# A transformer layer (linear attention, then eight experts) on one core, with every engine's calls in another order

## The reference, cut to what matters

```python
x = x + attn(layernorm(x), w_qkv, w_out)      # q, k with rope, then elu + 1; 16 heads of 16
#   kv = kv + k_t v_t ; ks = ks + k_t ; out_t = (q_t kv) / max(q_t ks, 1e-6); out @ w_out
x = x + ffn(layernorm(x), Wg, Wu, Wd, Wr, temperature)
#   weights = routing(sigmoid(x @ Wr / temperature))      # [rows, 8]
#   h = silu(x @ Wg[e]) * (x @ Wu[e]);  out = sum_e weights[:, e] * (h @ Wd[e])
```

## Time and profile before

| | before |
|---|---|
| median of 3 runs | 814.94 us |
| profiled execution, own time | 814.5 us |
| its span | 812.8 us |
| mean granted TensorE clock | 0.958 |
| TensorE busy (matmul) | 736.8 us, 91% |
| VectorE busy | 627.6 us, 77% |
| ScalarE busy | 493.6 us, 61% |
| GpSimd busy | 451.9 us, 56% |
| chain that ended last | PE 47%, DVE 22%, ACT 13%, issue 9%, POOL 5%, DMA 2% |
| x rows: issue to landing | 2.5 us (xr), 2.7 us (xa) |
| slabs: issue to landing | 4.0, 4.4, 3.7 us (Wg, Wu, Wd) |

### The profile page before, as it was taken

The page is one execution under the profiler, slowest core; times in us unless marked ns, Lnnn a source line. Parts: engine busy times, 40 slices in busy tenths (PEclk is TensorE's granted clock), DMA queues, the critical chain, the costliest instruction groups (busy, mean ns, idle before and its releaser), DMA issues.

```text
span 812.8 us, 18197 instructions
## 1 busy us (share of the span) xinstructions
PE 736.8 (91%) x6670; PEld 477.5 (59%) x6670; DVE 627.6 (77%) x1639; ACT 493.6 (61%) x936; POOL 451.9 (56%) x527
## 2 busy tenths in 40 slices
PE   5355579998999999999999999999999999999997
PEld 3344346664666665666666666666566666665654
DVE  6577788997987779777887878877977888767443
ACT  4655866775666665666666676666666676645332
POOL 2555446674566656656556655665565666563222
PEclk9666589999999999999999999999999999999999
DMA  4843210112311113122212102122221111110000
GB/s 138 204 104 104 55 28 13 41 40 42 67 40 35 25 25 66 41 40 43 66 40 40 38 18 55 40 41 42 66 40 41 40 22 35 26 27 9 19 2 27
DMA packets 97321, 38.28 MB, mean 47 GB/s; under 512 B 74192, under 2 KB 96976, under 8 KB 97232
## 3 DMA queue, kind: packets, MB, share of 16 engines
q1 hardware_dynamic: 97232, 37.12, 21.2%
HBM read 16.13 MB, written 4.19 MB: 25 GB/s over the span
## 4 chain that ended last, share of the span: by engine, by line
PE 47%; DVE 22%; ACT 13%; issue 9%; POOL 5%; DMA 2%; SPq 1%; DVEq 1%; ACTq 0%; POOLq 0%
PE up L460 13%; PE y L494 10%; PE gate L460 10%; PE front L333 5%; ACT L686 4%; POOL rop L1210 3%; DVE rop L862 3%; PE front L334 2%; DVE xa L1126 2%; ACT qk L564 2%; DVE q_st L878 2%; ACT work L686 2%; PE back L416 2%; DVE am L887 2%; DVE work L1113 2%
## 5 line engine op out<-in xcount | busy, mean ns | idle before, releaser
L1259 POOL TENSOR_TENSOR h_lo<-work,h_hi 128x512 f16<-128x512 f32 x128 | 148.6, 1161 | 68.7 <-ACT h_hi L693 68.7
L1231 POOL TENSOR_TENSOR a_lo<-am,a_hi 128x512 f16<-128x512 f32 x120 | 142.9, 1192 | 77.2 <-ACT a_hi L619 76.4
L1113 DVE SCALAR_TENSOR_TENSOR work<-up,ch,work 128x512 f32<-128x512 f32 x128 | 95.2, 744 | 62.5 <-PE up L460 62.2
L494 PE MATMUL y<-wd_hi,h_hi 128*128 128x256 f16 x512 | 139.5, 273 | 3.9 <-DVE xa L1126 3.7
L494 PE MATMUL y<-wd_hi,h_lo 128*128 128x256 f16 x512 | 139.5, 272 | 0.0
L494 PE MATMUL y<-wd_lo,h_hi 128*128 128x256 f16 x512 | 139.5, 272 | 0.0
L693 ACT ACTIVATE h_hi<-work 128x512 f16<-128x512 f32 x128 | 80.2, 627 | 62.4 <-DVE work L1113 40.9
L1126 DVE SCALAR_TENSOR_TENSOR xa<-y,wo,xa 128x256 f32<-128x256 f32 x256 | 113.5, 470 | 3.7 <-PE y L494 3.7
L686 ACT ACTIVATE work<-gate,isc 128x512 f32<-128x512 f32 x128 | 87.1, 681 | 26.1 <-POOL h_lo L1259 13.0
L619 ACT ACTIVATE a_hi<-am 128x512 f16<-128x512 f32 x120 | 74.8, 624 | 41.0 <-DVE am L887 40.3
L460 PE MATMUL up<-x_hi,wu_hi 128*128 128x512 f16 x256 | 77.1, 383 | 9.0 <-DVE work L1113 5.8
...
## 6 DMA issues: line engine op xcount, KB each, us to landing
...
qT<-q_st SPq DMA_TRANSPOSE x32, 3.2
```

The lines of the kernel that those rows point to most:

```text
L494: m = pe.matmul(Y[t // 2][:, t % 2 * D:(t % 2 + 1) * D], h_p[hi][:, n % 2, t * P:(t + 1) * P], wd_p[wi][:, u // KI, u % KI, :], start=(n % ...
L1113: v.scalar_tensor_tensor(out=hb[:, n % 2, :], in0=U[:, :], scalar=ch[:, e_:e_ + 1], in1=hb[:, n % 2, :], op0=ALU.mult, op1=ALU.mult).then_ ...
L1231: pool.tensor_tensor(a_p[1][:, heads(r), :], am_place(g, r).rearrange("p (h n) -> p h n", h=4), a_p[0][:, heads(r), :], ALU.subtract).then ...
L1259: pool.tensor_tensor(h_p[1][:, n % 2, :], hb[:, n % 2, :], h_p[0][:, n % 2, :], ALU.subtract).then_inc(s_hlo, 1)
```

## The change

Four things change in the text, and no operation of the computation is added or dropped.

- The head of every engine is written in another order.
- In the loop each engine's calls stand in another order. On TensorE `down(n - 1)` moves to directly behind `down(n - 2)`, and the second half of `scores(a)` moves to the step's end. On VectorE `o_sum(c)` no longer has `scale` between its halves in step 5, and the last `mask` goes behind `route_out`.
- The squares of slabs 12 to 23 leave the head and are done on ScalarE in step 5 (`late`).
- SP's head is written out transfer by transfer: x rows stand ahead of slabs, and slabs no longer stand between a transpose and the rows behind it. `load_xa` gets a wait on `s_bn`.

```diff
+LATE_SQUARES = 12
+        def late(s, i):
+            return LATE_SQUARES + i if s == LAG else None
...
@@ tensor_program, loop @@
-                logit_rows(router); gate(n); logit(router); up(n); qkv(a); gate(n + 1); av(c); down(n - 2)
+                logit_rows(router); gate(n); logit(router); up(n); qkv(a); gate(n + 1); av(c); down(n - 2)
+                down(n - 1)
                 if s == LAG:
                     totals(HEAD_BATCHES)
-                up(n + 1); down(n - 1); o_T(c); state(c); gate(n + 2); proj(c); up(n + 2); gate(n + 3); down(n)
-                scores(a, 0); scores(a, 1); x2_T(c); down(n + 1); up(n + 3)
+                up(n + 1); o_T(c); state(c); gate(n + 2); proj(c); up(n + 2); gate(n + 3); down(n); scores(a, 0)
+                x2_T(c); down(n + 1); up(n + 3); scores(a, 1)
...
@@ scalar_program, loop @@
-                x_hi(a + 1); slab_hi(slab(s, 0)); lg_copy(router); a_hi(c, 2); silu(n); a_hi(c, 3); h_hi(n - 1)
-                th(router); qk_copy(a); slab_hi(slab(s, 1)); fb(router); v_copy(a); e1(router); exp(a); silu(n + 1)
-                q_hi(a); k_hi(a); h_hi(n); v1(a); o_hi(c); h_hi(n + 1); silu(n + 2); slab_hi(slab(s, 2)); s1(c)
-                v2(a); slab_hi(slab(s, 3)); s2(c); x2_hi(c); a_hi(a, 0); h_hi(n + 2); silu(n + 3); a_hi(a, 1)
+                squares(late(s, 0)); squares(late(s, 1)); squares(late(s, 2)); squares(late(s, 3)); x_hi(a + 1)
+                squares(late(s, 4)); squares(late(s, 5)); slab_hi(slab(s, 0)); squares(late(s, 6)); lg_copy(router)
+                squares(late(s, 7)); a_hi(c, 2); slab_hi(slab(s, 1)); silu(n); th(router); a_hi(c, 3); h_hi(n - 1)
+                slab_hi(slab(s, 2)); e1(router); qk_copy(a); squares(late(s, 8)); v_copy(a); squares(late(s, 9))
+                squares(late(s, 10)); slab_hi(slab(s, 3)); squares(late(s, 11)); fb(router); exp(a); silu(n + 1)
+                k_hi(a); o_hi(c); q_hi(a); h_hi(n); v1(a); silu(n + 2); h_hi(n + 1); silu(n + 3); v2(a); s1(c)
+                x2_hi(c); s2(c); a_hi(a, 0); a_hi(a, 1); h_hi(n + 2)
...
@@ vector_program, loop @@
-                mask(c, 2); acc(n - 4, 0); bn(a + 1); slab_lo(slab(s, 0)); mask(c, 3); route_sum(router)
-                mean_var(a + 1); tcos_scale(a); x_lo(a + 1); acc(n - 4, 1); acc(n - 4, 2); acc(n - 4, 3)
-                var_eps(a + 1); route_zone(router); route_nearest(router); cos(a); h_up(n); rope(a)
...
+                mask(c, 2); acc(n - 4, 0); mask(c, 3); route_sum(router); tcos_scale(a); acc(n - 4, 1); x_lo(a + 1)
+                route_zone(router); h_up(n); acc(n - 4, 2); acc(n - 4, 3); slab_lo(slab(s, 0)); route_nearest(router)
+                route_weight(router); cos(a); bn(a + 1); o_sum(c, 0); rope(a); o_sum(c, 1); den_max(c)
+                route_first(router); mean_var(a + 1); den_rec(c); phi(a); slab_lo(slab(s, 1)); norm(c)
+                slab_lo(slab(s, 2)); route_second(router); route_tie(router); acc(n - 2, 0); acc(n - 2, 1); o_lo(c)
                 if s == LAG:
                     totals_kept(HEAD_BATCHES)
+                q_lo(a); h_up(n + 1); k_lo(a); x1_add(c); bn2(c); mean_var2(c); var_eps(a + 1); var_eps2(c)
+                slab_lo(slab(s, 3)); acc(n - 2, 2)
...
+                mask(a, 0); x2_lo(c); route_out(router); mask(a, 1); h_up(n + 3)
...
@@ gpsimd_program, loop @@
-                a_lo(c, 2); a_lo(c, 3); sin(a, 1); sin(a, 0); h_lo(n - 1); rstd1_pow(a + 1)
+                a_lo(c, 2); a_lo(c, 3); sin(a, 1); sin(a, 0); h_lo(n - 1); h_lo(n); v_rest(a)
                 if s == LAG:
                     inv_norm(HEAD_BATCHES)
-                v_rest(a); h_lo(n); h_lo(n + 1); rstd2_pow(c); st_rest(c)
-                s3(c); a_lo(a, 0); v3(a); a_lo(a, 1); h_lo(n + 2)
+                h_lo(n + 1); rstd2_pow(c); st_rest(c); v3(a); rstd1_pow(a + 1); s3(c); a_lo(a, 0); a_lo(a, 1)
+                h_lo(n + 2)
...
@@ sync_program, head @@
-            load_wqkv(0); load_wqkv(1)
-            load_xr(0); load_xa(0); load_xr(1)
...
+            load_wqkv(1); load_wqkv(0); load_wr(); load_xr(0); load_xa(0); load_tab(0); load_xa(1); load_slab(0)
+            load_xa(2); load_xr(1); load_xr(2); load_slab(1); load_xa(4); load_slab(2); load_xa(3); load_slab(3)
+            load_xr(3); load_xa(6); load_slab(4); load_slab(12); load_slab(5); load_slab(15); load_temp()
+            load_slab(6); transpose_q(0); transpose_k(0); load_slab(7); load_tab(1); load_slab(8); load_slab(9)
...
```

More of the change, by code:

```diff
@@ L1142, in vector_program @@
-            ln2(0); rope(3); mask(2, 1); den_rec(1); mean_var(5); norm(1); x_lo(4); phi(3); x2_lo(0); totals_kept(2)
-            mask(2, 2); slab_lo(3); mask(2, 3); q_lo(3); tcos_scale(4); o_lo(1); k_lo(3); cos(4); x1_add(1); bn2(1); mean_var2(1); var_eps2(1)
-            o_sum(2, 0); o_sum(2, 1); ln2(1); den_max(2); slab_lo(4); den_rec(2); st_add(2); wr_lo()
-            norm(2); scale(2); mask(3, 0); mask(3, 1); slab_lo(5); x2_lo(1); rope(4); o_lo(2); totals_kept(3); mask(3, 2); mask(3, 3); phi(4)
```

128 lines of the change are left out of this document (57 added, 71 removed).

## The result

| | before | after |
|---|---|---|
| median (4 runs each) | 815.02 us | 795.38 us (794.43 to 797.85) |
| ratio, 95% interval | | 0.9764 (0.9742 to 0.9786) |
| profiled execution, own time | 814.5 us | 797.85 us |
| its span | 812.8 us | 796.0 us |
| mean granted TensorE clock | 0.958 | 0.958 |

The forecast was 788.4 us in a range of 779 to 802: the sign and the range held, and 7 us of the expected gain did not come.

What follows compares the result with a forecast made beforehand. TensorE was taken to bound the kernel past the head, and VectorE's work and idle time the head. 814.5 - 16 - 3.0 - 5.5 - 6.0 + 4.0 = 788.0 us, with 0.4 for the median 788.4, range 779 to 802.

Steps and rivals of the forecast that it cites:

- The head: Up to logit_rows: 16 us earlier, at 83 us, by removing VectorE idle time, 4.6 of 20.6 us left; bounds 6 and 21.
- Rival 1: The head gives only 6 us, so the run takes 798.4 us; chance 0.18.
- Step 5: From logit_rows to the next qkv: -4.5 + 0.9 + 0.6 = -3.0 us; bounds -4.5 and +5.1.
- and this 4.5 goes: In step 5: TensorE's 4.52 us wait for norm(4) disappears, as both halves of o_sum(4) stand ahead of scale(4).
- 0.9 was counted: In step 5: 0.9 us lost as totals(4), with up(1) behind it, waits for the last square on ScalarE.
- the power, counted at 0.6: In step 5: GpSimd's pow of 2.28 us, now ahead of h_lo(1) and rstd2_pow(4), partly hidden, costs 0.6 us.
- Rival 4: Squares fall on step 5 in full, +8 us, and half of the 5.5 is lost: 799 us; chance 0.05.
- Steps 6 to 8: 5.5 of 6.1 us lost come back, as up(14) no longer waits for slab 22's low half; bounds 2.9 and 6.1.
- Later batches: Six steps beginning a batch beside a front gain 1.0 us each from shorter h_up and acc waits: -6.0; bounds 0 and -8.
- 7.7 / 7 = 1.1 us a batch: In later batches: TensorE's waits for h_up and acc, without one at the end, spread over seven batches.
- The cut of scores: One more full-height to half-height matmul change on TensorE in 27 steps, 0.15 us each: +4.0 us.
- Rival 3: down(n - 1) waits for GpSimd's late h_lo, 1.0 us or more in each of 27 steps, losing the whole gain; chance 0.05.

Runs made afterwards that it cites:

- second run of after: The changed kernel run and profiled again with no edit: 795.88 us, ratio 0.9764.
- experiment 3: The old kernel with only SP's transfers in the head rewritten as in the change: 808.81 us, ratio 0.9919.
- experiment 7: The changed kernel with each of the twelve squares in step 5 reading 32 of 512 columns: 795.78 us, ratio 0.9754.
- experiment 9: The changed kernel with GpSimd's power of twelve columns, and VectorE's scale and unscale, later in step 5: 795.84 us, ratio 0.9769.
- experiment 4: The changed kernel with VectorE's route_nearest and route_weight moved from ahead of cos(a) to behind den_max(c): 787.06 us, ratio 0.9657.
- Experiment 6: The old kernel with ScalarE's o_hi(c) ahead of h_hi(n) and VectorE's o_lo(c) ahead of q_lo(a) and k_lo(a): 818.41 us, ratio 1.0038.
- experiment 5: The changed kernel with the second half of scores(a) directly behind the first again on TensorE: 804.02 us, ratio 0.9858.
- experiment 11: The changed kernel with the halves of scores together and VectorE's st_add(c) moved to behind o_lo(c): 800.10 us, ratio 0.9814.
- experiment 10: The changed kernel with down(n - 1) behind up(n + 1) again on TensorE: 800.86 us, ratio 0.9833.

## Why the prediction was right, and where it was not

**The head: right in kind, 16 predicted and 14.1 measured** (12.8 in the second run of after). The new order of the transfers gave 6.2 (experiment 3); the rest came with the order of the calls and the twelve squares gone from the head, which no run parts. VectorE's remaining idle time behind 28.5 us is 5.4 us against the 4.6 that the step had. Rival 1 (6 us, 798.4) is out.

**Step 5: failed.** The step was "-4.5 + 0.9 + 0.6 = -3.0", and it came to +1.0 (+0.2 in the second profile). The wait of 4.52 us is gone from the profile, but the sentence "and this 4.5 goes" took TensorE's wait for what the move could give. These are `norm(4)` on VectorE of before and of after:

```profile
115.40 0.42 DVE L940 SCALAR_TENSOR_TENSOR nat<-osb,rec 128x256 f32<-128x256 f32 x1
```
```profile
99.62 0.42 DVE L946 SCALAR_TENSOR_TENSOR nat<-osb,rec 128x256 f32<-128x256 f32 x1
```

From `logit_rows` that is 16.43 and 14.78 us: `norm(4)` came 1.65 us sooner, not 4.5. Before, `scale(4)` and `unscale(1)` stood between the halves of `o_sum(4)`:

```profile
110.17 0.57 DVE L905 TENSOR_REDUCE osb<-back 128x136 f32<-128x408 f32 x1
112.65 0.18 DVE L760 TENSOR_SCALAR sc<-pw 128x12 int32<-128x12 int32 x1 [1.91 <-POOL pw L1176]
...
113.40 0.58 DVE L905 TENSOR_REDUCE osb<-back 128x136 f32<-128x408 f32 x1
```

They held the second half up from 110.74 to 113.40. These 2.7 us are all that moving them could take from `norm(4)`. The rest of the way to it is mostly VectorE's own work: 12.69 us busy of the 16.43 before, 12.96 of the 14.78 after. In the new order VectorE also waits there for GpSimd's `a_lo` (0.45 us), for `th` (0.73) and for `qk_copy(5)`:

```profile
95.51 0.70 DVE L858 TENSOR_TENSOR front<-front,tcos 128x512 f32<-128x512 f32 x1 [0.45 <-ACT qk L570]
```

`qk_copy` comes 7.97 us after `logit_rows` before and 9.90 after. About half of these 1.9 us is that `qkv(5)` itself ends 0.96 later. The other half is ScalarE's table load of 1.28 us: it came with `fb` at 107.65, behind `qk_copy`, and now comes with `e1` at 93.31, ahead of it. With the squares cut to 32 columns (experiment 7) `qk_copy` still comes at 9.89 and `norm(4)` at 14.75, so the squares delay neither. VectorE had other work in the meantime and lost only the 0.45 us to it. This is read from the traces; neither the table load nor VectorE's order was tried alone.

The rest of the sum, for the first profile: `o_T(4)` started 0.48 us after `norm(4)` before and 1.61 after, since `totals(4)` waits for the last square and `up(1)` stands behind it. That is 1.1 where 0.9 was counted; without the squares it is 0.47 again (experiment 7). The granted clock up to `o_T(4)` was 0.81 in after and 0.91 in experiment 7, so a part of the 1.1 is the slower clock. The part behind `o_T(4)` is 1.5 longer than before, both at a clock of 0.89; the power, counted at 0.6, is 1.1 of it by experiment 9. Together -1.65 + 1.13 + 1.48 = +0.96. Rival 4 (the squares fall on the step in full) is out: their absence changes the run's time by nothing that is measured.

**Steps 6 to 8: right**, 4.35 of 5.5 (3.56 in the second profile, at 69.53 us); no wait for `wu_lo` is left and the clock is 1.00 there. Step 8 alone takes 23.65 us where it took 28.30. Step 6 takes 23.06 (23.87) where it took 22.09, and the new waits in it are one of 1.26 us (1.19) for `kT` and, in the second profile, one of 0.76 for `h_lo`. No experiment was made on these three steps.

**Later batches: the mechanism right, and undone by another.** "7.7 / 7 = 1.1 us a batch" went as said: the waits for `h_up` and `acc` fell, and the operations of `route_out` got fast. In experiment 4 four steps of a batch take 23.01 + 22.21 + 21.65 + 21.60 = 88.47 us, against 90.35 before. Of these 1.9 us 0.8 are the 0.21 by which each step is shorter, and 1.0 is left for the router. But the change also put `route_nearest` and `route_weight` in front of `cos`, beside `sin` and `h_lo`, and there they cost 1.6 us a batch. The prediction had the mechanism in hand, and looked at one of the places where small operations meet GpSimd, not at the others.

The Trainium skill (page "SBUF — State Buffer", section "Who interferes with whom") says that a VectorE instruction with two inputs in this memory and a GpSimd instruction that reads it block each other for the whole instruction. The traces agree: L1037 takes 1.19 us beside an `h_lo` of 1.16 us, and 0.18 beside an idle GpSimd. By that rule every place in the order where small operations and a GpSimd call meet had to be priced, not the one that had got better.

**The cut of scores: the term was nearly right, and it bought something that was not seen.** The two halves take 0.33 us each against 0.55 together, and the `up` ahead of the second half 0.52 against 0.43 to the next group's start. That is 0.20 us for the 0.15 taken; 0.05 of it come back in the `down` in between (1.31 for 1.36). The way back, which the prediction found nowhere in the trace, was there in part: before, the second half is followed by `x2_T` after 0.31 us, where the first takes 0.24. The cut allows `st_add` to stand late, so that `o_lo` and `h_up(n + 1)` both come early, and the stretch from gate to `up(n + 2)` takes 2.01 us where it took 2.36. That is -0.35 + 0.20 - 0.05 = -0.20, the difference between 21.82 and 21.61 but for 0.01. Experiment 6 (`o_lo` early alone), experiment 5 (together, `st_add` late) and experiment 11 (together, `st_add` early) each do one part, and each loses. The wait was in the trace before, in the rows of the weight loads, which the prediction had not read:

```profile
PEld back L416 <- DVE ox_lo L948: 15.4, 26, 0.7
```

**Rival 3: its margin was 0.2 us, and it held.** GpSimd's `h_lo(n - 1)` in a plain step of after, and TensorE's `down(n - 1)`:

```profile
259.96 1.16 POOL L1262 TENSOR_TENSOR h_lo<-work,h_hi 128x512 f16<-128x512 f32 x1
```
```profile
261.31 0.27 PE L499 MATMUL y<-wd_hi,h_hi 128*128 128x256 f16 x1
```

`h_lo` ends at 261.12, 0.2 us ahead, where the earlier trace rows had 1.5. Taking the move back (experiment 10) leaves the plain step as it is. In step 6 the margin did not hold: in the second profile TensorE waits 0.76 us there for `h_lo` ahead of `down(n - 1)`.

The profiled execution lies 9.8 us above the 788.0 that the sum gave for it: 4.0 in step 5, 1.9 in the head, 1.15 in steps 6 to 8 and 2.7 from step 9 on. In the last, six hold-ups of 1.6 us (9.5 us that no term had) and the wait of 1.44 us for `kT` stand against -0.35 in each step, which no term had either. Experiment 4, with the hold-ups taken away, has a median of 787.1.
